# Attention and feed-forward kernel on one core: first products of the second unit split by level, fill products after a branch, a wait ahead of the last product, and a new written order on five engines

## What is computed

```python
k = layernorm(x)                              # over the 256 channels
w = -exp(time_decay)
# scan over the 128 steps, for each sequence and channel:
#   y_t = (e1*aa + e2*v_t) / (e1*bb + e2)     weighted mean of v so far, weights exp(k)
x = x + y
n = layernorm(x)
g = (n @ gate_w.T) * gate_s                   # 256 -> 704
u = (n @ up_w.T) * up_s
x = x + ((silu(g) * u) @ down_w.T) * down_s   # 704 -> 256
```

## Time and profile before

| | us |
|---|---|
| median of 3 runs | 106.54 |
| lowest, highest | 106.52, 106.72 |
| profiled execution, own time | 105.73 |
| profiled execution, span | 103.8 |
| TensorE busy | 91.5 (88%) |
| ScalarE busy | 77.4 (75%) |
| VectorE busy | 77.0 (74%) |
| GpSimd busy | 68.0 (65%) |

### The profile page before, as it was taken

The page is one execution under the profiler, slowest core; times in us unless marked ns, Lnnn a source line. Parts: engine busy times, 40 slices in busy tenths (PEclk is TensorE's granted clock), DMA queues, the critical chain, the costliest instruction groups (busy, mean ns, idle before and its releaser), DMA issues.

```text
span 103.8 us, 1619 instructions
## 1 busy us (share of the span) xinstructions
PE 91.5 (88%) x484; PEld 75.0 (72%) x484; DVE 77.0 (74%) x121; ACT 77.4 (75%) x136; POOL 68.0 (65%) x97
## 2 busy tenths in 40 slices
PE   3999888929399999999999999999999999999800
PEld 3968878919298778777787888886877788888500
DVE  1587999999977898999999999996716222945230
ACT  4367999999954999999999999999577426465000
POOL 2029679969997994894898899645399504576000
PEclk9999999999958999999999999999999999999975
DMA  1999999998000000000014000005000000050050
GB/s 31 311 331 403 363 400 373 374 385 321 11 3 3 0 0 6 0 0 0 0 50 152 0 0 6 0 0 202 0 0 0 0 0 3 27 185 0 6 202 6
DMA packets 6475, 10.78 MB, mean 104 GB/s; under 512 B 576, under 2 KB 3648, under 8 KB 6336
## 3 DMA queue, kind: packets, MB, share of 16 engines
q1 hardware_dynamic: 6320, 10.62, 28.8%
q10 hardware_dynamic: 144, 0.03, 0.2%
HBM read 8.55 MB, written 2.10 MB: 102 GB/s over the span
## 4 chain that ended last, share of the span: by engine, by line
PE 64%; DVE 20%; issue 5%; ACT 4%; DVEq 1%; POOL 1%; POOLq 0%; ACTq 0%
PE ps_f L691 35%; PE ps_d L708 17%; DVE sbe L516 5%; DVE sbp L527 5%; PE ps_f L719 4%; DVE den L541 3%; PE ps_x L647 3%; DVE num L551 2%; ACT L348 2%; DVE xl L567 2%; PE ps_a L628 2%; PE ps_x L668 2%; DVEq L58 1%; PE ps_x L653 1%; PE ps_d L653 1%
## 5 line engine op out<-in xcount | busy, mean ns | idle before, releaser
L691 PE MATMUL ps_f<-xh,wgu_r 128*128 128x512 f32 (+1 forms) x94 | 30.3, 404 | 2.2 <-issue 2.0
L334 POOL TENSOR_TENSOR hl<-h,hh 128x512 fp32r<-128x512 f32 x20 | 25.7, 1295 | 8.7 <-ACT hh L450 8.5
L691 PE MATMUL ps_f<-xl,wgu_r 128*128 128x512 f32 (+1 forms) x94 | 29.0, 391 | 1.8 <-DVE xl L567 1.8
L582 DVE SCALAR_TENSOR_TENSOR h<-ps_f,vec,sil 128x512 f32<-128x512 f32 x20 | 14.9, 747 | 11.0 <-PE ps_f L691 5.6
L691 PEld LDWEIGHTS ps_f<-xl,wgu_r 128*128 128x128 f32 x94 | 17.8, 196 | 5.9 <-DVE xl L567 2.3
L691 PEld LDWEIGHTS ps_f<-xh,wgu_r 128*128 128x128 f32 x94 | 17.0, 198 | 6.0 <-issue 2.2
L439 ACT ACTIVATE sil<-ps_f,vec 128x512 f32<-128x512 f32 x20 | 13.6, 686 | 5.5 <-PE ps_f L691 5.3
L708 PE MATMUL ps_d<-hh,wd_r 128*128 128x512 f32 x40 | 16.3, 407 | 0.0
L708 PE MATMUL ps_d<-hl,wd_r 128*128 128x512 f32 x40 | 15.7, 393 | 0.0
L450 ACT ACTIVATE hh<-h 128x512 fp32r<-128x512 f32 x20 | 12.4, 625 | 3.5 <-DVE h L582 3.5
L719 PE MATMUL ps_f<-ident 128*128 128x128 f32 x78 | 11.2, 303 | 1.6 <-POOL ident L247 1.6
(11 more groups left out here) (78 smaller groups left out, 136.7 us busy)
## 6 DMA issues: line engine op xcount, KB each, us to landing
xt<-x_tok SPq DMA_DIRECT2D x8, 256.0 KB, 6.9
xc<-x_ch SPq DMA_DIRECT2D x4, 512.0 KB, 11.0
out_ch<-xc SPq DMA_DIRECT2D x8, 256.0 KB, 2.4
wgu<-w_gu SPq DMA_DIRECT2D x1, 1408.0 KB, 8.4
vc<-v_ch SPq DMA_DIRECT2D x2, 512.0 KB, 10.8
wd<-w_d SPq DMA_DIRECT2D x1, 768.0 KB, 10.7
vt<-v_tok SPq DMA_DIRECT2D x2, 256.0 KB, 5.3
vt<-v_tok SPq DMA_DIRECT2D x1, 512.0 KB, 9.6
```

The costliest lines, as they stand in the source:

```text
L334: nc.gpsimd.tensor_tensor(hl[:, m, :], h[:, n % HS, :], hh[:, m, :].bitcast(F32), ALU.subtract).then_inc(s_hl, 1)
L582: nc.vector.scalar_tensor_tensor(h[:, n % HS, :] if m < FULL else up, up, vec[r, V_US + m:V_US + m + 1], sil[r, n % 2, :], ALU.mult, ALU.m ...
L691: last = nc.tensor.matmul(ps_f[:, i % RING, ts], w, a, start=c == 0 and x is xh, stop=c == CC - 1 and x is xl)
```

## The change

- `product` takes `levels`, so that the high products (`xh`) and the low ones (`xl`) can be issued apart. For the columns of unit 1, `gate(0)` and `up(0)` are now `uph(0); gateh(0); gatel(0); upl(0)`, and `gate(1)` is `gateh(1); gatel(1)`. The test on `HALVED` is gone.
- In group 0 every product now waits on `s_xh` and `s_xl`, where before only the first did.
- `fill(5)`, five identity products into a bank of `ps_d` that nothing reads then, stands first behind the branch. The number of `warm` products falls from 39 to 34.
- `downb(23)`, the last product, waits for a new semaphore `s_pace`, set by the high/low pair of `down(22)` for channel half 0.
- The lists of all five engines are written in another order. Among the places: `count` stands ahead of `e_T(3)`; `publish` ahead of `stats2(1)` and `scan_p(2)`; `low_n(1)` ahead of `numer(3)`; `high_n(0)` behind `norm2(1)`; and both `expk(4)` and `expk(5)` ahead of `high_n(1)`. `weigh(3)` stands ahead of `divide(1)`. `e_T(7)` moves ahead of `up(8)`. Loads of x from unit 4 on come later.

```diff
-HALVED = 3
...
+        s_pace = sem("s_pace")
...
-            load_x(0); load_x(1); load_x(2); load_x(3); load_v(0); load_v(1); load_wgu(); load_x(4); load_v(2)
-            load_wd(); load_x(5); load_res(0); load_x(6); load_res(1); load_x(7); load_res(2); load_v(3); load_res(3)
-            load_v(4)
+            load_x(0); load_x(1); load_x(2); load_x(3); load_v(0); load_v(1); load_wgu(); load_v(2); load_wd()
+            load_res(0); load_x(4); load_x(5); load_x(6); load_v(3); load_res(1); load_x(7); load_v(4); load_res(2)
+            load_res(3)
...
-            bias1(0); bias1(1); lead(0); weigh(0); bias1(3); weigh(1); lead(1); whi(0); divide(0); weigh(2); whi(4)
+            bias1(0); bias1(1); weigh(0); bias1(3); weigh(1); lead(0); lead(1); whi(0); divide(0); weigh(2); weigh(3)
...
-            def product(n, part, exact, half=None):
+            def product(n, part, exact, half=None, levels=(0, 1)):
...
-                if half == 0 or m == 0:
-                    pe.wait_ge(s_xh, units)
+                check = half is not None or m == 0 or g == 0
...
-                for x in (xh, xl):
-                    if x is xl and (half == 0 or m == 0):
-                        pe.wait_ge(s_xl, units)
+                for k in levels:
+                    x = (xh, xl)[k]
+                    if check:
+                        pe.wait_ge((s_xh, s_xl)[k], units)
...
-                        last = nc.tensor.matmul(ps_f[:, i % RING, ts], w, a, start=c == 0 and x is xh,
-                                                stop=c == CC - 1 and x is xl)
-                if half != 0:
+                        last = nc.tensor.matmul(ps_f[:, i % RING, ts], w, a, start=c == 0 and k == 0,
+                                                stop=c == CC - 1 and k == 1)
+                if half != 0 and 1 in levels:
...
+                if n == GROUPS * MC - 1 and 1 in chunks:
+                    pe.wait_ge(s_pace, 1)
...
+                    elif n == GROUPS * MC - 2 and c == 0:
+                        last.then_inc(s_pace, 1)
...
+            def fill(k):
+
+                for _ in range(k):
+                    nc.tensor.matmul(ps_d[:, 1, 0:P], ident[:, :], ident[:, :], start=True, stop=True)
...
-                gatea(0); upa(0); n_T(1); p_T(3); gatea(1); e_T(4); gate(0); x1_T(2); up(0); gate(1); up(1); gate(2)
...
+                fill(5); n_T(1); p_T(3); gatea(0); upa(0); gatea(1); e_T(4); uph(0); gateh(0); gatel(0); upl(0)
+                gateh(1); gatel(1); x1_T(2); up(1); gate(2); up(2); gate(3); up(3); n_T(2); gate(4); gate(5); x1_T(3)
...
-            warm(10); x_T(0); x_T(1); warm(3); e_T(0); warm(7); p_T(0); e_T(1); warm(10); p_T(1); e_T(2); y_T(0)
-            warm(1); p_T(2); warm(8); y_T(1); e_T(3); count(); n_T(0)
+            warm(8); x_T(0); warm(6); e_T(0); warm(7); p_T(0); e_T(1); x_T(1); warm(5); p_T(1); e_T(2); y_T(0)
+            warm(1); p_T(2); warm(7); y_T(1); count(); e_T(3); n_T(0)
```

More of the change, by code:

```diff
@@ L452, in high_h @@
                     nc.scalar.activation(hx[REST:P, :], ps_f[REST:P, slot(n, 1) % RING, :], ACT.Copy).then_inc(s_hh, 1)
-            rstd1(0); expk(0); rstd1(1); elift_(); rstd1(3); expk(1); expk(2); log_den(0); expk(3); recip(0)
-            wcheck(0); log_den(1); wcheck(1); recip(1); rstd2a(0); wcheck(2); norm2(0); rstd1(5); log_den(2)
-            high_n(0); rstd2a(1); recip(2); norm2(1); expk(4); high_n(1); log_den(3); expk(5); recip(3); tables(SILU)
+            rstd1(0); rstd1(1); expk(0); elift_(); rstd1(3); expk(1); expk(2); log_den(0); expk(3); recip(0)
@@ L457, in _ @@
+            wcheck(0); log_den(1); wcheck(1); recip(1); rstd2a(0); wcheck(2); norm2(0); log_den(2); rstd1(5)
+            rstd2a(1); recip(2); norm2(1); high_n(0); expk(4); expk(5); log_den(3); high_n(1); recip(3); tables(SILU)
             silu(0); silu(1); high_h(0); silu(2); high_h(1); norm2(2); silu(3); high_h(2); high_n(2); high_h(3)
-            silu(4); silu(5); tables(LN_EXP); log_den(4); rstd1(7); norm2(3); recip(4); expk(6); high_n(3); high_h(4)
-            log_den(5); high_h(5); recip(5); expk(7); tables(SILU); silu(6); silu(7); norm2(4); high_h(6); silu(8)
@@ L460, in _ @@
[L460 to L464, removed]
+            silu(4); silu(5); tables(LN_EXP); rstd1(7); log_den(4); norm2(3); recip(4); expk(6); high_n(3); high_h(4)
@@ new lines, in _ @@
+            log_den(5); high_h(5); expk(7); recip(5); tables(SILU); silu(6); silu(7); norm2(4); silu(8); high_n(4)
+            high_h(6); silu(9); high_h(7); tables(LN_EXP); log_den(6); high_h(8); recip(6); norm2(5); tables(SILU)
+            silu(10); high_n(5); silu(11); high_h(9); high_h(10); silu(12); high_h(11); tables(LN_EXP); log_den(7)
+            high_h(12); recip(7); tables(SILU); silu(13); silu(14); norm2(6); high_h(13); high_h(14); high_n(6)
+            silu(15); high_h(15); silu(16); norm2(7); high_h(16); high_n(7); silu(17); high_h(17); silu(18)
@@ L609, in _ @@
             stats1(0); stats1(1); stats1(2); lift_(); decay_(); stats1(3); scan_e(0); denom(0); scan_p(0); scan_e(1)
[L610 to L618, removed]
+            numer(0); denom(1); scan_p(1); numer(1); stats2(0); scan_e(2); stats1(4); denom(2); stats1(5); publish()
+            stats2(1); scan_p(2); scan_e(3); numer(2); denom(3); low_n(0); scan_p(3); stats1(6); low_n(1); numer(3)
+            scan_e(4); gated(0); stats2(2); gated(1); mulp(4); denom(4); gated(2); stats1(7); gated(3); low_n(2)
+            scan_p(4); stats2(3); numer(4); mulp(5); scan_e(5); gated(4); gated(5); denom(5); low_n(3); scan_p(5)
+            scan_e(6); low_rest(5); stats2(4); numer(5); gated(6); mulp(6); gated(7); denom(6); low_n(4); finish(0)
+            stats2(5); gated(8); gated(9); scan_p(6); numer(6); scan_e(7); gated(10); low_n(5); mulp(7); gated(11)
+            denom(7); low_rest(11); gated(12); stats2(6); scan_p(7); numer(7); gated(13); gated(14); finish(1)
+            low_n(6); gated(15); stats2(7); gated(16); gated(17); low_n(7); low_rest(17); gated(18); gated(19)
+            gated(20); gated(21); finish(2); gated(22); gated(23); low_rest(23); finish_c(0); finish_c(1)
         @block.tensor
@@ new lines, in rest_of_program @@
+                gateh(1); gatel(1); x1_T(2); up(1); gate(2); up(2); gate(3); up(3); n_T(2); gate(4); gate(5); x1_T(3)
+                e_T(5); down(0); down(1); up(4); down(2); n_T(3); down(3); e_T(6); gate(6); x1_T(4); up(6); down(4)
+                gate(7); down(5); up(7); gate(8); n_T(4); gate(9); e_T(7); up(8); x1_T(5); up(9); down(6); gate(10)
+                up(10); gate(11); n_T(5); down(7); down(8); gate(12); x1_T(6); up(12); down(9); gate(13); gate(14)
+                up(13); down(10); down(11); up(14); gate(15); n_T(6); up(15); gate(16); x1_T(7); up(16); down(12)
```

36 lines of the change are left out of this document (20 added, 16 removed).

## The result

The changed kernel takes 102.45 us in the median of 4 runs (102.29 to 102.68), the kernel before 106.53 us (105.94 to 106.72). The ratio is 0.963, with a 95% interval of 0.959 to 0.967. It is faster by 4.1 us. The forecast was faster by 2.0, with a range down to 103.7: the sign was right, the size was half, and the time lies outside the range.

The account below looks back on a forecast made before the run. Bound up to 28 us by something other than TensorE, then by TensorE nearly without pause; 31.36 - 29.6 + 0.26 = 2.0 us from the earlier long run, other terms 0, gave 106.54 - 2.0 = 104.5 us, range 103.7 to 106.0.

Parts of the forecast that it names:

- The branch and the fill: TensorE after n_T(0): flag at about 19.9, work again at 21.9 instead of 23.31, five fill products costing nothing.
- Unit 1 and the next wait: TensorE, unit 1: low products from 27.7 instead of 28.34; up(1) waits for silu(0), starting at 29.6 instead of 31.36.
- The clock: TensorE before unit 1's low products: shorter pauses keep 2.4 GHz; the slow clock had cost 1.67 us.
- The term of 2.0 us: TensorE's long run from up(1) on: ahead by 31.36 - 29.6 + 0.26 = 2.0 us, and staying so.
- the small later waits: Small waits of the kernel before, 0.17 and 0.08 us, said to go; 2.0 was kept.
- The wait ahead of the last product: TensorE's last product waits for down(22): no effect at the end, bounds -0.2 to +0.2 us, taken as 0.
- the 5.8 us of the end: From TensorE's last product to the program's end: expected to take the same 5.8 us as before.
- Earlier start of the scans: Front of the kernel: e_T(0) ready 0.4 to 0.7 us earlier, VectorE's 0.41 wait gone, 0.4 kept up to stats2(0).
- From one execution to the median: Whole kernel: the median lay 0.8 us above the profiled execution before, so 106.54 - 2.0 = 104.5 us.
- more than forecast: Rival at TensorE's up(1): silu(0) 0.45 us earlier plus 0.25 of small waits give 2.7 (103.8 us); chance 0.09.

Follow-up runs that it names:

- a_no_pace: The changed kernel without the wait on s_pace and without setting it; 104.04 us, beside 106.76 for the kernel before.
- a_no_fill: The changed kernel without fill(5); 102.82 us (kernel before 106.76), and again 102.78 against 102.20 for the changed kernel.
- a_unsplit: The changed kernel with unit 1's columns as whole products, high and low together; 102.56 us (kernel before 106.76), and again 102.34 against 102.47 for the changed kernel.
- b_pace: The kernel before with only the wait on s_pace and its signal added; 105.30 us, 1.5 below the kernel before.
- b_fill_pace_start: The kernel before with fills in its two pauses, the s_pace wait and the changed kernel's TensorE start; 102.77 us, against 103.60 without that start.

## Why the prediction was wrong

**The branch and the fill** were right. The flag came at 20.40 (19.9 forecast), the first matmul behind the branch at 21.68 (21.9), and a pause of 0.70 was left behind the fill, so it cost nothing. That 21.9 came so close is partly luck: the flag was 0.5 late, and the prediction added the 1.3 us of the branch to the end of `n_T(0)`, which it put at 20.6. In both traces they lie behind the flag (21.92 to 23.31, 20.40 to 21.68), and the pause behind `n_T(0)` was only 0.33.

**Unit 1 and the next wait** were right within 0.4 us. `low_n(1)` ran at 27.28 (27.0), the low products at 28.12 (27.7), `up(1)` at 29.95 (29.6), directly behind `silu(0)` and its table load, and with no pause on TensorE behind it.

**The clock** stayed up as forecast. The term of 2.0 us measured 1.88 in the profiled pair. Here too luck helped: at the first full product only 1.6 of it was there (low pair at 30.50 against 32.09), and most of the rest fits the small later waits that the prediction named (0.17 and 0.08) and did not add. Of the gain behind `n_T(0)`, about 1.5 is the clock and 0.5 the lists.

**The wait ahead of the last product** is the step that failed. The prediction gave it "-0.2 to +0.2, taken as 0", reasoning only with TensorE, the semaphore and VectorE. The runs show 1.2 to 1.5 us (`a_no_pace` 1.2 and 1.5 above `a_no_fill` and `a_unsplit`, which keep the wait and shared its chip, `b_pace` 1.5 below the kernel before), by way of an instruction fetch on a DMA engine that the output needed. The row that held it was there: the landing of the last output took 3.6 us of SyncE's waiting, and the 5.8 us of the end were carried over as a constant and not taken apart. In the profiled pair the forecast span was 101.8 and the measured one 100.5; this step is that difference of 1.3 us, to within 0.1. On the weight loads, the prediction feared that the wait would take their overlap; the row at 95.44 shows both loads ahead as before, so the rule of the Trainium skill (TensorE: Matmul & The Clock Gate, on what happens when a matmul is issued) is not contradicted, and the wait cost that load nothing.

**Earlier start of the scans** was half right. The prediction took the 0.41 us wait for `e_T(0)` to vanish; it grew to 0.85, because the clock rose later in this execution, and `scan_e(0)` started 0.18 later instead of 0.4 earlier. But `b_fill_pace_start` shows 0.8 us in the median for that very edit. The profiled execution of before started earlier (`scan_e(0)` at 8.45) than all five traces of variants built on it (9.02 to 9.84), and so hid how much the cold start usually costs.

**From one execution to the median** the prediction added 0.8 us to both sides. In the changed kernel only 0.16 remained. A late first rise and a second fall, which the change makes cheaper or removes, would explain the rest, but these runs do not divide it. The prediction had dismissed the spread that the Trainium skill's free-running monitor (same page, on the clock gate) would bring, since three runs lay within 0.2 us. Across four groups the kernel before spread from 103.6 to 109.2 in three separate bands of clock, and the page's rule agrees with that. Three close runs had not excluded it.

Against the rivals: "more than forecast" had the right side and the wrong place. Its mechanism, an earlier `silu(0)`, did not occur.

The whole, from same-chip medians: the fills gave 1.8 us (106.44 to 104.65), the wait with the fills 2.6 (106.23 to 103.60), the start on TensorE 0.8 more, and the remaining lists with the split 0.3. That leaves 0.8 us for the wait in this sum, while its single tests give 1.2 to 1.5. The traces, where start and clock can be taken out, decide for the latter: 1.5 for the clock, 0.5 for the lists, 1.1 to 1.4 for the wait. What stays open is the share of the start.

## What to carry to other kernels

Cut the traces of all variants at the same few events, and compare the stretches rather than the ends: that told a chance start from a gain here, where medians could not. Take the end of the span apart like any other stretch: compare the landing of the last output with that of the others, and look for instruction packets inside it, above all where an engine jumps over code that is not run. Before taking a profiled execution as the base of a sum, ask which of its stretches depend on chance, the moment of the first clock rise and the place of a fall, since a change can be worth more in the median than in that execution. An unread product in a pause costs nothing where the engine waits anyway, and it can be worth more than a better order.

## What was not expected of the hardware

- With one instruction packet of about 16 KB inside the last 512 KB of output, SyncE waited 3.5 to 3.6 us for the output instead of 2.0 to 2.2, and the last few packets arrived singly, 6 to 8 in a microsecond.
- A wait on one engine changed the time of the program by over 1 us without moving any product: it moved that engine's instruction fetch.
- A fall of the clock does not have one price. With the lists of the kernel before it cost 1.4 to 1.6 us, at 28 us in continuous work (as read there, 1.67) and at 24 us between two pauses alike. In the changed kernel without its fill it cost 0.1 to 0.2 us at 24 and 0.6 to 0.7 at 26.
